# A two-layer attention, expert and recurrent-cell kernel: output products placed behind the cell's last steps, earlier first keys, a bias split over four rounds, new orders and lags

## The reference

```python
x = x + xattn0(layernorm(x), ctx, ctx)   # 16 heads of 8, q/k/v/out biases
x = x + experts(layernorm(x))            # 8 experts, top 2 by gate score, weighted by the scores themselves
x = x + xattn1(layernorm(x), ctx, ctx)   # 16 heads of 8, no biases
x = x + cell(layernorm(x))
```

```python
def step(c, xt):
    ft = sigmoid(xt @ wf.T + c @ uf.T + bf)
    it = sigmoid(xt @ wi.T + c @ ui.T + bi)
    gt = tanh(xt @ wc.T + c @ uc.T + bc)
    return ft * c + it * gt
c_final = scan(step, c0, x)
h = tanh(x @ wo.T + c_final @ uo.T + bo)
```

## Time and profile before

| | us |
|---|---|
| median of 3 runs | 868.63 |
| lowest, highest | 867.02, 868.85 |
| the profiled execution's own time | 869.94 |
| its span in the trace | 868.2 |
| PE busy | 836.5 (96%) |
| DVE busy | 789.6 (91%) |
| ACT busy | 782.3 (90%) |
| POOL busy | 624.0 (72%) |

### The profile page before, as it was taken

The page is one execution under the profiler, slowest core; times in us unless marked ns, Lnnn a source line. Parts: engine busy times, 40 slices in busy tenths (PEclk is TensorE's granted clock), DMA queues, the critical chain, the costliest instruction groups (busy, mean ns, idle before and its releaser), DMA issues. The chain is left out here.

```text
span 868.2 us, 41445 instructions
## 1 busy us (share of the span) xinstructions
PE 836.5 (96%) x15262; PEld 745.8 (86%) x15262; DVE 789.6 (91%) x2965; ACT 782.3 (90%) x2488; POOL 624.0 (72%) x1098
## 2 busy tenths in 40 slices
PE   5699999999999999999999999999999999999887
PEld 3488899999999999999999999999999999898765
DVE  4789999999999999999999999999999999999834
ACT  4699999999999999999999999999999999888754
POOL 4777887777877787777777777778777877766514
PEclk9999999999999999999999999999999999999999
DMA  9400000000000000000000000000000000000005
GB/s 337 165 3 2 3 3 4 3 4 3 3 3 3 3 3 4 3 3 4 3 4 3 3 4 3 3 4 3 4 3 3 3 3 4 3 4 2 3 2 194
DMA packets 6822, 17.68 MB, mean 20 GB/s; under 512 B 736, under 2 KB 2016, under 8 KB 6624
## 3 DMA queue, kind: packets, MB, share of 16 engines
q1 hardware_dynamic: 6336, 14.50, 4.4%
q10 hardware_dynamic: 288, 0.53, 0.2%
HBM read 10.84 MB, written 4.19 MB: 17 GB/s over the span
## 5 line engine op out<-in xcount | busy, mean ns | idle before, releaser
L1072 POOL TENSOR_TENSOR h<-Ex 128x512 f32<-128x512 f32 (+1 forms) x144 | 165.9, 1152 | 43.0 <-ACT Ex L613 42.4
L806 DVE TENSOR_REDUCE mx<-ps 128x8 f32<-128x512 f32 (+1 forms) x288 | 173.4, 623 | 14.5 <-PE ps L308 13.7
L820 DVE TENSOR_TENSOR Ex<-ps,mx 128x512 f32<-128x512 f32 (+1 forms) x288 | 172.7, 620 | 0.0
L323 PE MATMUL ps<-w,Ex 128*128 128x128 f32 x1024 | 164.0, 278 | 4.4 <-DVE Ex L820 2.9
L624 ACT ACTIVATE ET<-ps 128x512 f32<-128x512 f32 (+1 forms) x288 | 163.4, 567 | 1.2 <-PE ps L323 0.9
L613 ACT ACTIVATE Ex<-Ex 128x512 f32<-128x512 f32 (+1 forms) x288 | 164.4, 597 | 0.0
L1056 POOL TENSOR_TENSOR rs<-ve,half 128x4 f32<-128x4 f32 (+3 forms) x77 | 70.4, 914 | 128.5 <-DVE ve L796 125.8
L930 DVE SCALAR_TENSOR_TENSOR acc<-ps,we,acc 128x128 f32<-128x128 f32 x448 | 151.8, 339 | 6.0 <-PE ps L409 3.4
L662 ACT ACTIVATE hT<-ps,w 128x128 f32<-128x128 f32 x512 | 147.1, 382 | 3.4 <-PE ps L388 2.9
L388 PEld LDWEIGHTS ps<-xT,w 128*128 128x128 f32 x1024 | 124.2, 191 | 24.6 <-issue 24.6
L409 PE MATMUL ps<-w,hT 128*128 128x128 f32 x1024 | 141.8, 281 | 1.1 <-DVE Ex L820 1.0
(11 more groups left out here) (105 smaller groups left out, 1800.3 us busy)
## 6 DMA issues: line engine op xcount, KB each, us to landing
out_dram<-x SPq DMA_DIRECT2D x15, 256.0 KB, 2.7
cx<-ctx_dram SPq DMA_DIRECT2D x7, 512.0 KB, 12.7
x<-x_dram SPq DMA_DIRECT2D x7, 512.0 KB, 13.6
w<-weights_dram SPq DMA_DIRECT2D x2, 576.0 KB, 7.6
w<-weights_dram SPq DMA_DIRECT2D x1, 512.0 KB, 5.4
w<-weights_dram ACTq DMA_DIRECT2D x1, 264.0 KB, 3.7
w<-weights_dram ACTq DMA_DIRECT2D x1, 256.0 KB, 3.2
cx<-ctx_dram SPq DMA_DIRECT2D x1, 256.0 KB, 5.5
```

Source lines behind the costliest of these rows:

```text
L323: m = e.transpose(b[:, 128 * n:128 * n + 128], Ex[:, j % 2, r, 128 * n:128 * n + 128], ident)
L806: e.tensor_reduce(mx[:, j % 2, r, 4 * lo:4 * hi], b[:, 256 * lo:256 * hi].rearrange("p (j k) -> p j k", k=64), AX.X, ALU.max).then_inc(sig ...
L820: e.tensor_tensor(Ex[:, j % 2, r, 256 * lo:256 * hi].rearrange("p (j k) -> p j k", k=64), b[:, 256 * lo:256 * hi].rearrange("p (j k) -> p ...
L1072: e.tensor_tensor(u, v[:, :, :, 0:32], v[:, :, :, 32:64], ALU.add).then_inc(sig("half1"), 1)
```

## The change

The diff changes eight things:

- L2 and L3 become 9 and 14 (attention 1 and the cell start one round later), FIRST becomes -1, and many lags move: the out projection, three transposes of the exponentials, the sums, and the second half of the experts' output come one round later.
- The order of the calls in the loops of PE, ACT, DVE and POOL, and the table USES, are new.
- Keys and values of tile 0 are made in round 0 instead of 1; those of tile 1 stay in round 2.
- `bias_pieces` runs two operations at the start of each of the rounds 0 to 3. The biases b2 move from the fifth weight block (w4, SP's queue) to the third (w2, ACT's queue).
- `out_inputs` is called twice a round from round 73 on: nine groups go to SBUF, the next five are the first five input shares of the end, each in the bank where the end uses it (`ENDS`). Before the first of them PE waits for all bank readers except `turnx`.
- After the loop only the bias matmuls, c_final's product and the cell shares are left, with the inputs of the last two PE groups.
- TAIL gives 28 tiles to PE (seven groups instead of eight), 28 to POOL, and 8 to DVE, which adds the cell's part to all four of its pairs ahead of its first residual add.
- POOL's `halves(1)` comes before `halves(0)` of the same tile.

```diff
-NW = 8
-TAIL = [("dve", 0, 2), ("pe", 32, 4), ("pool", 2, 4), ("pe", 36, 4), ("pool", 6, 4), ("pe", 40, 4), ("pool", 10, 4),
...
+TAIL = [("dve", 0, 2), ("pe", 36, 4), ("pool", 2, 4), ("pe", 40, 4), ("pool", 6, 4), ("pe", 44, 4), ("dve", 30, 2),
+        ("pool", 10, 4), ("pe", 48, 4), ("pool", 14, 4), ("dve", 32, 2), ("pe", 52, 4), ("pool", 18, 4),
+        ("pe", 56, 4), ("pool", 22, 4), ("pe", 60, 4), ("pool", 26, 4), ("dve", 34, 2)]
+NW, EARLY = 9, 5
...
-L1, L2, L3 = 5, 8, 13
+L1, L2, L3 = 5, 9, 14
...
-FIRST, LAST = 0, NT + 16
+LAST_STEP = NT + L3 - 1 + LAG["sB"]
+FIRST, LAST = -1, NT + 16
...
+        last = bank_of("turnx", NT + L3 - 1)
+        ENDS = [b for b in banks[0:7] if b is not last] + [last, lstm]
...
             def keys_values(i):
                 t = i - LAG["kv"]
-                if not on(t):
+                if t == 0 or not -1 <= t < NT:
                     return
                 b = bank(i, "kv")
+                t = max(t, 0)
...
+            def out_inputs(i, u):
+                g = 2 * (i - LAST_STEP + 6) + u
+                if not 0 <= g < NW + EARLY:
+                    return
+                if g >= NW:
+                    inputs_share(g - NW)
+                    return
...
+            def inputs_share(m):
+                lo = TAIL[MINE[m]][1]
+                if m == 0:
+                    for name, reader, _, chain, step, first in USES:
+                        if name != "turnx":
+                            e.wait_ge(sig(reader), step * (SPAN[chain][1] - 1) + first)
...
             for i in range(FIRST, LAST):
+                experts(i, 1)
+                project(i)
                 step(i, 1)
+                turn_e(i, 3)
+                turn_e(i, 1)
                 gate(i)
                 turn_w(i)
                 turn_r(i)
-                out_inputs(i)
+                out_inputs(i, 0)
                 hidden(i, 0)
...
+                turn_e(i, 0)
+                turn_x(i)
+                expert_bias(i)
+                out_inputs(i, 1)
                 experts(i, 0)
                 query(i)
-            inputs_share(0)
...
-            for m in range(1, 5):
-                inputs_share(m)
...
-                if i == FIRST + 6:
-                    bias_pieces()
+                if FIRST + 1 <= i < FIRST + 5:
+                    bias_pieces(2 * (i - FIRST) - 2)
+                    bias_pieces(2 * (i - FIRST) - 1)
...
+            for adder, lo, n in TAIL:
+                if adder == "dve":
+                    e.tensor_tensor(cx[:, lo:lo + n, :], cx[:, lo:lo + n, :],
+                                    ENDS[6][:, 0:128].unsqueeze(1).to_broadcast([P, n, 128]),
+                                    ALU.add).then_inc(sig("pre_dve"), 1)
```

More of the change, by code:

```diff
@@ L433, in out_inputs, with cell_share @@
                                  skip_group_check=True)
-                m.then_inc(sig("wx"), 1)
+                m.then_inc(sig(f"wx{u}"), 1)
+            def inputs_share(m):
[4 more added lines that the diff above has]
+                            e.wait_ge(sig(reader), step * (SPAN[chain][1] - 1) + first)
+                if m >= EARLY:
+                    e.wait_ge(sig("out"), MINE[m - EARLY] + 1)
+                e.wait_ge(sig("xT"), lo + 4 + L3)
+                for n in range(4):
+                    e.matmul(end_bank(MINE[m])[:, 128 * n:128 * n + 128], cx[:, lo + n, :], wT[:, WX, :], start=(n == 0),
+                             stop=False, skip_group_check=True)
+            def cell_share(m):
+                e.matmul(end_bank(MINE[m])[:, :].rearrange("p (t d) -> p t d", t=4), ident,
+                         cU[:, :].unsqueeze(1).to_broadcast([P, 4, 128]), start=False, stop=True,
+                         skip_group_check=True).then_inc(sig("pre_pe"), 1)
             def cell_inputs(i):
@@ L498, in tensor_program @@
                 values(i)
+                turn_e(i, 0)
+                turn_x(i)
+                expert_bias(i)
+                out_inputs(i, 1)
                 experts(i, 0)
-                turn_e(i, 3)
-                turn_x(i)
-                turn_e(i, 0)
-                experts(i, 1)
-                project(i)
-                query(i)
-            for _, reader, _, chain, step, first in USES:
-                e.wait_ge(sig(reader), step * (SPAN[chain][1] - 1) + first)
-            for n in (6, 5):
-                e.matmul(banks[n][:, 0:128], ident, bo1, start=True, stop=False, skip_group_check=True)
-            inputs_share(0)
+                query(i)
+            for n in (5, 6):
+                e.matmul(ENDS[n][:, 0:128], ident, bo1, start=True, stop=False, skip_group_check=True)
             e.wait_ge(sig("C"), 2 * NT + 1)
@@ L515, in tensor_program @@
                 for g in (0, 64):
-                    m = e.matmul(banks[n][g:g + 64, 0:128], c_end, wT[:, UO, :], start=False, stop=True,
+                    m = e.matmul(ENDS[n][g:g + 64, 0:128], c_end, wT[:, UO, :], start=False, stop=True,
                                  skip_group_check=True)
                 m.then_inc(sig("uo"), 1)
-            for m in range(1, 5):
-                inputs_share(m)
             e.wait_ge(sig("cU"), 1)
-            for m in range(len(mine)):
-                if m >= 5:
+            for m in range(len(MINE)):
+                if m >= EARLY:
                     inputs_share(m)
@@ L713, in scalar_program @@
                 turn_e(i, 0)
+                turn_x(i)
+                out_inputs(i, 0)
+                exps(i, 1)
+                exps(i, 0)
+                query(i)
+                out_inputs(i, 1)
                 widen(i)
                 gates(i, 1)
[L716 to L724 removed]
+                turn_e(i, 3)
+                turn_e(i, 1)
+                turn_w(i)
+                turn_r(i)
+                exps(i, 2)
+                exps(i, 3)
+                relus(i, 0)
+                turn_e(i, 2)
+                scale(i)
                 relus(i, 1)
[L726 removed]
                 gates(i, 0)
                 keys_values(i)
[L729 to L732 removed]
             e.wait_ge(sig("uo"), 1)
[L734 to L735 removed]
+            e.activation(cU[:, :], ENDS[5][:, 0:128], ACT.Copy).then_inc(sig("cU"), 1)
+            begun = {"dve": 0, "pe": 0, "pool": 0}
             for k, (adder, lo, n) in enumerate(TAIL):
[L737 to L745 removed]
+                begun[adder] += 1
+                e.wait_ge(sig("pre_" + adder), begun[adder])
+                dst = end_bank(k)[:, 512 - 128 * n:512].rearrange("p (t d) -> p t d", t=n)
+                if adder != "pe" and SIDE.index(k) >= 2:
+                    e.wait_ge(sig("out"), SIDE[SIDE.index(k) - 2] + 1)
+                e.activation(dst, dst if adder == "pe" else cx[:, lo:lo + n, :], ACT.Tanh).then_inc(sig("tanh"), 1)
         def vector_program(e):
```

184 lines of the change are left out of this document (71 added, 113 removed), and 28 rows, old and new, of tables (LAG, USES).

## The result

The changed kernel takes **921.9 us** (median of 4 runs, 921.63 to 922.24), the kernel before 867.97 (4 runs, 867.02 to 868.85). The ratio is 1.0622, interval 1.0603 to 1.064: 54 us slower, where 16.5 us faster was forecast, with a range of 845 to 861 us. The profiled execution has 922.24 us and a span of 920.4.

The account below looks back on a forecast made before the run. PE was taken to bound the full rounds, with DVE nearly as full. Gains of 8.5, 1.3, 0, 3.5 and 3.4 us sum to 16.7, rounded down to 16.5: 868.63 us becomes 852.1, range 845 to 861.

Parts of the forecast that it names:

- It stays below PE: Full rounds: DVE gets c2, c3, c4 in a row; one more neighbour is 0.12 us against a wait of at least 0.21.
- (2): Rival: full rounds become PE's and DVE's together, slower than before; 878 us at 0.5 us per round; chance 0.04.
- What would show it: List of signs to check; for (2), the gate's wait on DVE gone and PE idle time in each round.
- Full rounds: Middle of the kernel: 12.25 us a round instead of 12.28, 1.3 us gained over 52 rounds.
- The start: First rounds: bias block gone, half clock gone, light rounds shorter; 8.5 us gained, between 5 and 10.5.
- The bias term: Start: DVE's bias block goes, its eight operations standing in rounds 0 to 3 where DVE waits; 3.95 us gained.
- The half clock: Start: the round of 8.06 us takes 6.2 at full clock; 1.9 us gained, bounds nothing and 2.8.
- the term of the light rounds: Start: the new order shortens rounds from scores to scores to 5.2 us; 2.6 us gained, bounds 0 and 4.
- The last rounds: Cell's last rounds: 2.5 us gained less 1.1, 1.0 and 0.5 us; about zero, within 2.5 us.
- So they cost nothing there: Last rounds: groups of output products fill PE waits of 1.23 to 1.49 us; 1.1 us counted in rounds 73 to 76.
- the first early share: Last rounds: PE's wait for the copy of group 8 puts 1.0 us on the chain, once; bounds 0 and 2.
- Behind the last step: After the last sB: c_final's product 2.9 us later, 3.5 us gained; then 15.7 us to the end, 3.4 us gained.

Follow-up runs that it names:

- repaired version: The changed kernel with one edit: POOL's sum of the gate weights again comes before its second pair of head sums; 857.59 us, ratio 0.9881.
- experiment 4: A kernel without the computation: DVE's short operations run beside POOL's additions, small powers, one-input copies and memsets in turn; run once, cast up to an addition's length.
- experiment 11: Against the 860.61 us version (narrow wait, all even output copies a round sooner): nine groups of output products four rounds sooner; 871.68 us, ratio 1.0048.
- experiment 9: The repaired version with the five early shares of the output inputs back behind the last step; 862.23 us, ratio 0.9947.
- experiment 3: The kernel before, with DVE's cast and gate weights moved and POOL's second half sums ahead of its gate sum, so that they collide; 901.38 us, ratio 1.0383.
- experiment 10: The repaired version with DVE's eight bias operations in one piece in the seventh round, as before; 863.16 us, ratio 0.9956.
- experiment 5: The changed kernel with DVE's cast early in the round and the weights left behind the experts' statistics; 859.78 us, ratio 0.9908.
- experiment 7: The repaired version with the first early share's wait narrowed and ACT's output copies a round sooner: all even groups 860.61 us, second version, last group alone, 855.58 us.
- Experiment 6: The repaired version with PE's first early share waiting only for the last reader of its own bank; 855.78 us, ratio 0.9873.

## Why the prediction was wrong

**The failed step is "It stays below PE"**, under the full rounds. DVE was costed as 12.0 us plus 0.12 for one more neighbour, with each operation at its length in the old order. Two operations took 1.57 us more in the new one. DVE is busy 578.59 us in the 49 full rounds of the repaired version, 11.8 each; 11.8 + 1.57 = 13.37, and the rounds of the changed kernel measured 13.38 (13.2 of them busy on DVE, with no wait for another engine). The rival that came true is (2), the full rounds becoming DVE's, which had a chance of 0.04. It was right in kind (it decides from a DVE round of 12.6); its price was far short (878 us), and its mechanism was another: no wait of c1 or c6 appeared. On DVE the gate's wait is gone, as "What would show it" says of that case.

The profile of before had the sign of it, in the bias block. Its first subtraction took four times as long as its second:

```profile
35.47 1.16 DVE L955 TENSOR_TENSOR w<-w,b2p 72x128 f32<-72x128 f32 x1
...
37.32 0.29 DVE L955 TENSOR_TENSOR w<-w,b2p 72x128 f32<-72x128 f32 x1
```

```profile
35.44 1.04 POOL L1029 TENSOR_TENSOR Km<-kT,w 128x512 f32<-128x512 f32 x1
```

I counted the block as a whole, 4.19 us, and took its length for that of its work. The Trainium skill (SBUF — State Buffer, Who interferes with whom) states the rule: a DVE instruction in a two-port mode, which copies and casts can enter, excludes any GpSimd instruction, one with two inputs in SBUF excludes a GpSimd instruction that reads SBUF, and the one that comes later waits for the whole of the other. The traces agree for the cast and the weights (1.20 and 0.75 us), and disagree beside POOL's small power, which reads SBUF, is recorded with 1.0 us, and held nothing (0.20 us in experiment 4).

**Full rounds** without the hold: 12.16 us, forecast 12.25. The direction was right and the size too small: 0.12 us in 49 rounds are 5.9 us, not 1.3 (the forecast counted 52 rounds). Which part of the new order gave it no run shows. "I am wrong if full rounds move by more than 0.05 us" holds in both directions.

**The start**, forecast 8.5 us by the sixth scores. PE's timeline of the changed kernel:

```profile
24.77 1.09 PE L319 MATMUL ps<-Km,qT 32*64 32x256 f32 x16 [0.34 <-issue]
...
30.63 0.30 PE L345 MATMUL ps<-w,rd 128*128 128x128 f32 x1 [0.99 <-ACT rd L649]
...
31.60 0.69 PE L319 MATMUL ps<-Km,qT 32*64 32x256 f32 x16 [0.35 <-ACT rT L662]
...
37.51 0.69 PE L319 MATMUL ps<-Km,qT 32*64 32x256 f32 x16 [0.35 <-ACT rT L662]
...
44.67 0.69 PE L319 MATMUL ps<-Km,qT 32*64 32x256 f32 x16
```

The sixth scores start at 44.67, before at 48.74: **4.1 us** gained (44.94 and so 3.8 in the repaired version). The bias term was right: 9.77 - 5.91 = 3.86 us, forecast 3.95. The half clock went with the block, as forecast, but gave less: the round behind it is 44.67 - 37.51 = 7.16 us where it was 8.06, so 0.9 us, forecast 1.9. What failed is the term of the light rounds, 2.6 us: they did not shrink to 5.2 but are 6.83 and 5.91 us (24.77, 31.60, 37.51), where before they were 5.82, and with the 0.3 us won ahead of 24.77 this term is a loss of 0.7. In the first of them POOL's clearing of `Vb`, 1.80 us, delays the half sums and so the reciprocal. Before, the same instruction ran at 33.55 beside the bias block, where PE stood anyway:

```profile
26.26 1.80 POOL L1146 MEMSET Vb<- 128x2048 f32 x1
28.14 0.73 POOL L1089 TENSOR_TENSOR h<-Ex 128x256 f32<-128x256 f32 x1
```

Removing a stall brought into the open what it had covered. (This is read from the traces; no run moved the clearing.) The clock can also fall in the start without any bias block, as in the repaired version:

```profile
24.00:31.00 7.00, 6.82 (x80) 5.25 (x80) 4.21 (x14) 4.18 (x16) 5.51 (x7) 0.54 0.95 380
```

The changed kernel has full clock there, and yet the seventh scores stand at 52.65 in the one and at 52.94 in the other: so early, half clock costs little.

**The last rounds**, forecast zero. In the repaired version the last sB starts at 836.76, so 5.85 us sooner than before. The start gives some 4.6 us by the seventh scores (57.53 and 52.94) and the full rounds 5.9; the last rounds and the moved order therefore lose about 4.6. Two terms were too small. "So they cost nothing there", said of the products in the cell's last rounds, holds for one group a round (four instructions, eight rows of the trace) and not for two: the last four rounds take 25.0 us instead of 21.3, and experiment 11 puts the second group at 0.3 to 1.0 us in three of them, where 1.1 us was forecast for all. And the first early share costs the chain 1.75 us (experiment 9), not 1.0; PE waits 1.92 us ahead of it. These are 3.7 and 1.75 us of loss, so the rounds ahead of them gained about 0.9, where 2.5 - 0.5 was forecast. PE's waits did not get fewer: from the end of the full rounds up to shortly before the last step it is idle 109.2 - 102.03 = 7.2 us, 5.0 before in a stretch of 98.1 us.

**Behind the last step** the forecast held. c_final's product starts 839.66 - 836.76 = 2.9 us behind the last sB (forecast 2.9), at full clock, and the end is 855.7 - 839.66 = 16.0 us later (forecast 15.7):

```profile
836.76 0.54 PE L492 MATMUL ps<-CG,w 128*32 128x64 f32 x24 [0.40 <-DVE CG L957]
837.23 2.05 PE L461 MATMUL ps<-w,cx 128*128 128x128 f32 x16
839.12 0.61 PE L524 MATMUL ps<-w 128*128 128x128 f32 x4
839.66 0.66 PE L530 MATMUL ps<-w,CG 128*64 128x128 f32 x8
840.48 4.56 PE L465 MATMUL ps<-cU,w 128*128 128x512 f32 x10 [0.16 <-ACT cU L749]
```

Together the repaired version gains 5.85 + 3.6 + 3.1 = 12.5 us of span, where 16.5 were forecast: 857.59 us lies in the range of 845 to 861. That the sum comes so near is partly luck: the full rounds gave 4.6 us more than forecast, the start 3.9 and the last rounds 4.6 less. What was missed is one interaction of two reorderings: it cost 64 us (921.9 and 857.59), where all the rest was worth 10.

## What to carry to other kernels

Where both DVE and POOL work all the time, an instruction's length belongs to its place: when an order changes on one of them, look at what now runs beside each DVE copy, cast and two-SBUF-input operation on the other, and price it up to the length of POOL's instruction. In a profile, look for one line whose instructions have different lengths at the same shape, and for ends that coincide with another engine's. Before counting a removed stall as gained, list what ran beside it.

## What the runs showed of the hardware that was not expected

- The hold doesn't depend on how small the DVE operation is: two numbers per partition waited 1.04 us. It lasts as long as POOL's instruction has left (0.60 us when the cast began in its middle). Beside a memset, which only writes, the cast was held too (0.95 us).
- POOL's power on 128x4 numbers, 1.02 us long, holds nothing: the weights beside it in the kernel before took 0.22 us.
- In the three kernels with the bias block in one piece the granted clock was low behind it (0.51 from 40.1 to 47.0 us before, 0.76 from 38 to 45 in experiment 3, 0.51 in experiment 10), in no other. Apart from that it fell somewhere between 17 and 38 us in eight versions and stayed full there in the kernel before, the changed kernel, experiment 5 and both versions of experiment 7. Experiment 6 and the second version of experiment 7 run the same instructions in the start; it fell in the one (0.57 from 17 to 24 us) and not in the other, so the program alone doesn't decide it. The seventh scores stand at 52.20 and 53.07 us, sooner where it fell.
- The semaphore waits ahead of the first share, one for each of 22 bank uses, cost PE 0.68 us (1.92 to 1.24) though ACT's copy, the last to be waited for, had ended 0.73 us before.
